# Centring the output weights on chip and dropping the mean from the norms behind them, in a two-layer attention and expert kernel on one core

## The reference, cut to what matters

```python
x = x + layernorm(attention(layernorm(x)))     # linear attention, 16 heads of 8, causal; ends in  values @ Wo + bo
x = x + layernorm(ffn(layernorm(x)))           # ffn = shared expert + top-1 of 16 experts
# shared:  (silu(h @ w_gate.T) * (h @ w_up.T)) @ w_down.T
# expert:  (up * silu(gate)) @ down_proj[e],   gate, up = split(score * h @ gate_up_proj[e])
# layernorm(y) = (y - mean(y)) / sqrt(var(y) + 1e-5), without gain or bias
```

## Time and profile before

| | us |
|---|---|
| median of three runs (lowest, highest) | 351.48 (351.32, 351.48) |
| the profiled execution: its own time | 353.47 |
| its span, first to last instruction | 351.6 |
| VectorE busy | 284.8 (81%) |
| TensorE busy | 266.0 (76%) |
| GpSimd busy | 193.1 (55%) |
| ScalarE busy | 188.8 (54%) |

### The profile page before, as it was taken

One profiled execution on the slowest core, in us unless ns is written; L12 is line 12 of the kernel. 1 busy time (PEld: TensorE's weight loads), 2 busy tenths in 40 slices (PEclk: granted clock), 3 DMA queues, 4 the chain that ended last, 5 costly groups with the idle time before them and its releaser, 6 DMA issues.

```text
span 351.6 us, 6328 instructions
## 1 busy us (share of the span) xinstructions
PE 266.0 (76%) x1493; PEld 189.3 (54%) x1493; DVE 284.8 (81%) x1147; ACT 188.8 (54%) x572; POOL 193.1 (55%) x221
## 2 busy tenths in 40 slices
PE   0449899999999995838887988730999999999100
PEld 0215565565656552524555755520999988988000
DVE  3599999999999999996998786560279999999940
ACT  1723566565656652447666563301799888885000
POOL 5064677777677773300055556371006888888870
PEclk9998999999999999877999899965699999999855
DMA  4999960000000000000011111126960101110100
GB/s 112 334 427 348 352 203 0 2 3 0 2 0 2 2 0 0 1 3 0 0 63 61 62 62 61 62 76 196 358 207 15 34 30 36 39 36 32 31 2 0
DMA packets 20275, 28.60 MB, mean 81 GB/s; under 512 B 2285, under 2 KB 15476, under 8 KB 19856
## 3 DMA queue, kind: packets, MB, share of 16 engines
q1 hardware_dynamic: 16624, 21.57, 18.2%
q0 software_dynamic: 3040, 6.37, 5.3%
q10 hardware_dynamic: 576, 0.26, 0.3%
HBM read 15.57 MB, written 13.60 MB: 83 GB/s over the span
## 4 chain that ended last, share of the span: by engine, by line
PE 39%; DVE 21%; POOL 17%; issue 12%; DMA 5%; ACT 1%; another core or an unknown queue 1%; SPq 1%; POOLq 0%; ACTq 0%; DVEq 0%
PE banks L1019 13%; POOL out L484 10%; POOL rows L478 5%; PE banks L1042 5%; DMA rows<-in_x 4%; PE banks L1106 3%; PE banks L1140 2%; PE banks L1048 2%; DVE hT L824 2%; POOL sorted_rows L468 2%; PE banks L1007 2%; PE banks L1040 1%; PE banks L1065 1%; PE banks L1063 1%; DVE stats L859 1%
## 5 line engine op out<-in xcount | busy, mean ns | idle before, releaser
L443 POOL TENSOR_TENSOR kv<-qk,vv 128x1024 f32<-128x1024 f32 x32 | 62.5, 1952 | 2.5
L1019 PE MATMUL banks<-kv,upto 128*128 128x512 f32 x128 | 61.3, 602 | 0.8 <-POOL kv L443 0.8
L1140 PE MATMUL banks<-xsT,w_now 128*128 128x128 f32 x376 | 53.8, 288 | 0.4 <-issue 0.4
L484 POOL DMA_INDIRECT out<-rows,token_i x47 | 46.9, 998 | 9.6 <-issue 8.0
L437 POOL TENSOR_TENSOR qk<-ex,rl 128x256 f32<-128x256 f32 x32 | 23.3, 729 | 50.4 <-ACT ex L542 50.4
L1140 PEld LDWEIGHTS banks<-xsT,w_now 128*128 128x128 f32 x376 | 48.1, 200 | 1.2 <-issue 0.5
L468 POOL DMA_INDIRECT sorted_rows<-rows,slot_i x32 | 31.6, 986 | 30.2 <-DVE slot_i L814 22.2
L728 DVE TENSOR_TENSOR prod<-banks,qk 128x1024 f32<-128x1024 f32 x32 | 38.9, 1217 | 2.7 <-PE banks L1019 0.8
L750 DVE TENSOR_REDUCE num<-prod 128x128 f32<-128x1024 f32 x32 | 38.7, 1208 | 0.3 <-DVE den L745 0.3
L958 DVE TENSOR_TENSOR hT_e<-silu_e,banks 128x256 f32<-128x256 f32 x47 | 19.3, 412 | 19.6 <-ACT silu_e L619 14.9
L478 POOL TENSOR_TENSOR rows<-rows,yn 128x128 f32<-128x128 f32 x40 | 19.2, 481 | 28.4 <-DVE yn L950 26.6
(11 more groups left out here) (152 smaller groups left out, 660.6 us busy)
## 6 DMA issues: line engine op xcount, KB each, us to landing
sorted_rows<-rows SPq DMA_DIRECT2D x3, 1950.0 KB, 12.0
rows<-sorted_rows SPq DMA_DIRECT2D x11, 520.0 KB, 6.2
w_exp<-in_gate_up SPq DMA_DIRECT2D x4, 1024.0 KB, 9.2
w_exp_down<-in_down SPq DMA_DIRECT2D x8, 256.0 KB, 8.8
out<-rows,token_i POOLq DMA_INDIRECT x47
rows<-in_x SPq DMA_DIRECT2D x1, 512.0 KB, 8.9
sorted_rows<-rows,slot_i POOLq DMA_INDIRECT x32
rows<-sorted_rows SPq DMA_DIRECT2D x1, 390.0 KB, 5.4
```

Of the source, the lines that this page charges most:

```text
L443: nc.gpsimd.tensor_tensor(kv[:, u, :].rearrange("p (h m d) -> p h m d", h=NH, m=HD), k, v, ALU.mult).then_inc(s_kv, 1)
L484: nc.gpsimd.indirect_dma_start(out=out_rows, out_offset=bass.IndirectOffsetOnAxis(ap=token_i[:, j - 1:j], axis=0), in_=rows[:, j - 1, 0:D] ...
L1019: ins = nc.tensor.matmul(ps_s[u % 2][:, cols], upto[:], kv[:, u, cols], start=True, stop=True)
L1140: ins = nc.tensor.matmul(ps_gue[u % 2][:, c * P:(c + 1) * P], w_now[:, u % 2, c * P:(c + 1) * P], xsT[:, u % 2, :], start=True, stop=True)
```

## The change

The means of `bo`, of the rows of `w_o`, of `w_d` and of all `w_exp_down` are subtracted on VectorE by `centre_steps` (a reduction over the 128 columns, then one scalar_tensor_tensor with the sum broadcast). The norm of the attention output and the norm of the ffn output then need only rstd. `ya`, `yn`, `nmean3` and the semaphores `s_ya`, `s_yn`, `s_fin_last` are gone. In stage 2 VectorE does the residual of each tile in one instruction, `x = y * rstd + x`, four of 128x128 in place of two additions of 128x256. In stage 3 it does the same for each output tile, and GpSimd only issues the output DMAs. The norm of a quad is `scale_steps`, 11 instructions in place of 14, and the outputs of a quad are made in the second half of the next quad's steps. The first norm's inputs keep their mean (`nmean2[:, 0]` is still made).

```diff
+def scale_steps(nc, series, st, width, scratch, rs):
+    mean_even, sq_even, sq_odd = st[1], st[2], st[5]
+    ve, y, t = scratch[0:3]
+    series.wait()
+    yield series.done(tensor(t, mean_even, mean_even, ALU.mult))
+    yield series.done(fused(out=ve, in0=sq_even, scalar=width * EPS, in1=sq_odd, op0=ALU.add, op1=ALU.add))
+    series.wait()
+    yield series.done(fused(out=ve, in0=ve, scalar=1.0 / width, in1=t, op0=ALU.mult, op1=ALU.add))
...
+    yield series.done(fused(out=rs, in0=t, scalar=0.5625, in1=y, op0=ALU.add, op1=ALU.mult))
+SCALE_STEPS = 11
+def centre_steps(nc, series, rows_of, sums, ready=None):
+    n, width = rows_of.shape[1], rows_of.shape[2]
+    yield series.done(nc.vector.tensor_reduce(sums, rows_of, AX, ALU.add))
+    series.wait()
+    ins = nc.vector.scalar_tensor_tensor(
+        out=rows_of, in0=sums.rearrange("p (n o) -> p n o", o=1).to_broadcast([P, n, width]), scalar=-1.0 / width,
+        in1=rows_of, op0=ALU.mult, op1=ALU.add)
+    yield ins.then_inc(ready, 1) if ready else ins
...
 # GpSimd, stage 3
-            for j in range(ST + 1):
-                if j < ADDED_BY_POOL:
-                    r = flat(rows[:, j:j + 1, 0:D])
-                    pool.wait_ge(s_yn, j + 1)
-                    nc.gpsimd.tensor_tensor(r, r, yn[:, j % 4, :], ALU.add).then_inc(s_fin, 1)
...
+            for j in range(ST):
+                pool.wait_ge(s_fin, j + 1)
+                nc.gpsimd.indirect_dma_start(
...
 # ScalarE, setup and stage 2
             act.wait_ge(s_bias, 64)
+            act.wait_ge(s_centred_o, 1)
...
-                if live(s + 3, NG):
-                    act.wait_ge(s_norm2, s + 4)
-                    for k in range(GT):
...
-                            ACT.Identity, bias=nmean2[:, 1, c], scale=rstd2[:, 1, c])
...
 # VectorE, setup
             dve.wait_ge(s_x[0], 16)
             setup.done(finish(stats_of(*CHUNKS[0])))
+            dve.wait_ge(s_bias, 64)
+            finish(centre_steps(nc, centring, bias[:, 3 * D:4 * D].rearrange("p (n d) -> p n d", n=1), row_sums[:, 0:1])
+                   ).then_inc(s_centred_o, 1)
...
             left_of_bias(1)
+            dve.wait_ge(s_w, 64)
+            finish(centre_steps(nc, centring, w_o[:].rearrange("p (n d) -> p n d", n=1), row_sums[:, 1:2])
+                   ).then_inc(s_centred_o, 1)
             dve.wait_ge(s_x[1], 16)
...
 # VectorE, stage 2, prepare_steps
-                    for half in range(2):
-                        dve.wait_ge(s_ya, 2 * (s + 2) + 1 + half)
...
+                    dve.wait_ge(s_norm2, s + 3)
+                    for k in range(GT):
+                        t = GT * (s + 2) + k
+                        x1 = flat(rows[:, tiles(t), 0:D])
+                        yield nc.vector.scalar_tensor_tensor(
+                            out=x1, in0=flat(rows[:, tiles(t), D:2 * D]), scalar=rstd2[:, 1, tiles(t)], in1=x1,
+                            op0=ALU.mult, op1=ALU.add).then_inc(s_x1, 1)
...
 # VectorE, attention step 4 and the hand-over
-            run_steps(dve, first_step1, 0, 4, 28, 28, 8, 4)
+            run_steps(dve, first_step1, 0, 4, 28, 4, 8, 4)
+            dve.wait_ge(s_w2, 64)
+            shared = centre_steps(nc, centring, w_d[:], row_sums[:, 0:FC], s_centred_d)
+            step1(4, 0, shared, 1)
+            run_steps(dve, step1, 5, 4, 28, 28, 8, 4)
...
+            dve.wait_ge(s_wexp, 16 * (E // 4) * (1 + FC))
+            for e in range(0, E, 4):
+                ins = finish(centre_steps(nc, centring, w_exp_down[:, e:e + 4, :, :].rearrange("p e c d -> p (e c) d"),
+                                          row_sums[:, e * FC:(e + 4) * FC]))
+            ins.then_inc(s_centred_e, 1)
 # VectorE, stage 3
+            def outputs(q, first, last):
+                dve.wait_ge(s_series3, SQ * (q + 1))
+                for i in range(4 * q + first, min(4 * q + last, ST)):
+                    x1 = flat(rows[:, tiles(i), 0:D])
+                    nc.vector.scalar_tensor_tensor(out=x1, in0=flat(rows[:, tiles(i), D:2 * D]),
+                                                   scalar=rstd3[:, q % 2, i % 4:i % 4 + 1], in1=x1,
+                                                   op0=ALU.mult, op1=ALU.add).then_inc(s_fin, 1)
...
+            for j in range(-4, 4 * QUADS):
+                q, u = j // 4, j % 4
+                step3(q, u)
+                if u == 0 and live(q - 1, QUADS):
+                    norms3 = norm_quad(q - 1, min(4, ST - 4 * (q - 1)), Series(dve, s_series3, SQ * (q - 1)))
+                last = q == QUADS - 1
+                for _ in range(((8, 4, 0, 0) if last else (4, 2, 2, 0))[u]):
+                    next(norms3, None)
+                half = u - (1 if last else 2)
+                if live(q - 1, QUADS) and half in (0, 1):
+                    outputs(q - 1, 2 * half, 2 * half + 2)
+            finish(norm_quad(QUADS - 1, ST - 4 * (QUADS - 1), Series(dve, s_series3, SQ * (QUADS - 1))))
+            outputs(QUADS - 1, 0, 4)
```

More of the change, by code:

```diff
@@ L923, in _, with norm_quad, step3 @@
             nc.vector.tensor_scalar(tile_expert[:], tile_expert[:], E - 1, None, ALU.bitwise_and).then_inc(s_experts, 1)
-            norms3 = {}
-            def step3(q, u, parity):
+            dve.wait_ge(s_wexp, 16 * (E // 4) * (1 + FC))
[3 more added lines that the diff above has]
+            ins.then_inc(s_centred_e, 1)
+            def norm_quad(q, n, norm):
+                c = tiles(4 * q, n)
+                dve.wait_ge(s_stats3, min(4 * (q + 1), ST))
+                yield nc.vector.tensor_scalar(token_i[:, c], rows[:, c, TOKEN], -1.0, float(NTOK), ALU.mult, ALU.add)
+                for ins in scale_steps(nc, norm, [stats3[:, 0:n, k] for k in range(6)], D,
+                                       [scratch3[:, k, 0:n] for k in range(3)], rstd3[:, q % 2, 0:n]):
+                    yield ins
+            def outputs(q, first, last):
[5 more added lines that the diff above has]
+                                                   op0=ALU.mult, op1=ALU.add).then_inc(s_fin, 1)
+            norms3 = iter(())
+            def step3(q, u):
                 j = 4 * q + u
@@ L933, in norm_step @@
                     for _ in range(count):
[L934 to L954 removed]
+                        next(norms3, None)
+                if j > 0:
+                    dve.wait_ge(s_sum, min(j, ST))
                 if live(j + 2, ST):
@@ L964, in step3 @@
                                        flat(rows[:, tiles(j - 1), D:2 * D])).then_inc(s_stats3, 1)
[L965 to L970 removed]
+                if u:
+                    norm_step()
                 if live(j, ST):
@@ L1103, in step2 @@
                     at_least(pe, s_sh_out, s)
+                    if s == 0:
+                        pe.wait_ge(s_centred_d, 1)
                     for k in range(GT):
```

97 lines of the change are left out of this document (32 added, 65 removed).

## The result

The changed kernel takes 368.38 us (median of 4 runs, 367.88 to 370.56); the kernel before took 351.40 beside it. The ratio is 1.0498, 95% interval 1.0455 to 1.0541: slower by 5%, where 336.4 us was forecast. The profiled execution took 367.88 us with a span of 366.0, 14.4 more than the span of before.

What follows compares the result with a forecast made beforehand. Stage 3 was taken as bound by VectorE and GpSimd, each holding the other. Terms -7.8 - 5.8 - 1.7 + 1.2 - 1.0 = -15.1 against 351.48 gave 336.4 us; range 333.5 to 339.5 (0.60), wider 331.5 to 342.5.

Steps and rivals of the forecast that it cites:

- Stage 3, pace: Stage 3's 32 tiles: GpSimd no longer a bound, 1.46 us a tile in place of 1.705; -7.8 us.
- Rival A: Stage 3: VectorE stays the bound at 1.59 us a tile, giving 340.6 us; chance 0.14.
- the terms ahead of stage 3: Before stage 3: setup -1.7 us, w_d centring +1.2, stage 2 -1.0, expert centring nothing.
- Stage 3, end: After the last gate and up products: GpSimd sets the end, 13.5 us in place of 19.3; -5.8 us.
- Setup and w_d: Setup: first attention product at 24.3 us, -1.7; attention step 4: w_d centring delayed by kv, +1.2 us.
- Stage 2: Stage 2: ScalarE's ya goes and four shorter instructions replace two additions; -1.0 us (-2 to +1.5).
- rival B: Setup and attention: kv meets the norms, +1.9 in place of -1.7, and w_d costs +2; 340.8 us, chance 0.12.
- Rival D: Stage 3: each output DMA is held by VectorE's new two-input instruction; 358 us if p = 1.89, chance 0.03.

Runs made afterwards that it cites:

- e10: Kernel before with GpSimd's four additions of a quad first, then its four output DMAs in a row, on chip C: 384.23 us, 1.076 of the kernel before.
- e18: The kernel after, unchanged, run again on chip A: 341.97 us, 0.973 of the kernel before.
- e13: Kernel after with a GpSimd addition ahead of each output DMA but the last seven, without w_d's centring, chip D: 354.26 us, 1.003 of the kernel before.
- e4: Kernel before with GpSimd's four additions of a quad first, then its four output DMAs in a row, on chip A: 352.48 us, 1.003 of the kernel before.
- e1: Kernel after with outputs made one in each step (pairs in the last quad), on chip A: 342.91 us, 0.977 of the kernel before.
- e2: Kernel after with GpSimd starting its output DMAs only when all outputs are made, on chip A: 398.53 us against 350.21 for the kernel before.
- e3: Kernel after with one GpSimd addition of its own ahead of each output DMA but the last seven, on chip A: 350.07 us, 0.9995 of the kernel before.
- e17: Kernel after with every token's index past the output's end, so the same DMAs store nothing, on chip A: 342.67 us against 351.28 for the kernel before.
- e16: Kernel before with all of the change but its part in stage 3, on chip D: 355.24 us, 1.012 of the kernel before.
- e15: Kernel after with outputs sent by SyncE's queue in sorted order, without centring bo and w_o, on chip D: 330.29 us, 0.935 of the kernel before.
- e11: Kernel after with outputs made one in each step (pairs in the last quad), on chip C: 362.38 us, 1.014 of the kernel before.
- e14: Kernel after with one output a step and a GpSimd addition ahead of each output DMA but the last seven, chip D: 354.99 us, 1.005 of the kernel before.
- the first three runs: e1, e2 and e3, variants of the kernel after on chip A: 342.91, 398.53 and 350.07 us.

## Why the prediction was wrong

**The step that failed** is the first, "Stage 3, pace": "GpSimd falls from 1.65 to 1.29 us a tile: no longer a bound." GpSimd is no bound, as said, but I took its DMAs out of the reckoning once it had time for them, and put at nothing, without a reason, what four of them in a row do to the waits of the other engines. On the chips of the comparison, B and C they hold TensorE's signals, and the pace goes to 2.18 and more in place of 1.46: +15.2 us over 32 tiles where -7.8 was forecast, and +2.3 in the stretch ahead of them, where the first row of DMAs falls. The addition L478, which I booked as pure cost (0.48 us a tile), also kept the DMAs 1.66 to 1.85 us apart; e10 takes that distance from the kernel before, and on chip C it stands at 1.076 of it.

**The reckoning of the pace was right where nothing is held.** e18 on chip A: (316.64 - 270.02) / 32 = 1.457 us a tile (1.46 forecast), 46.6 us for the 32 tiles in place of 54.6, which is the -7.8 forecast, to 0.2. VectorE is busy 44.02 of 48 us there, 1.34 a tile, where I had summed 1.38. TensorE is full, as forecast. Rival A (VectorE stays the bound) is out. Yet the whole of e18 is 9.3 us under the kernel before (351.28), not 15.1: -7.9 and -4.9 in stage 3 come to -12.8, and some 3.5 us are lost ahead of them. That 341.97 lies inside the range forecast is in part luck, for the terms ahead of stage 3 were wrong.

**Stage 3, end**: 28.4 before, 23.5 in after's profile and in e18: -4.9 in both, where -5.8 stood (-4.8 to -7). Right in kind, at the edge of its range.

**Setup and w_d.** Forecast -1.7 and +1.2 up to the first attention products. The first product indeed starts at 25.28 in place of 26.62 (24.9 forecast), but the fourth at 41.06 in place of 39.88. I counted only up to the first product; the norms of the last chunk go on through the next three steps and meet `kv` there. The timeline of after, third step of GpSimd's `kv`:

```profile
28.25 1.95 POOL L482 TENSOR_TENSOR kv<-qk,vv 128x1024 f32<-128x1024 f32 x1
...
28.41 1.82 DVE L101 TENSOR_SCALAR scratch<-scratch 128x20 int32<-128x20 int32 x1
```

How many do differs from run to run: over the sixteen profiles with the centrings of `bo` and `w_o` the first product starts from 25.28 to 27.53 (26.2 in the mean) and the fourth from 39.72 to 44.30 (41.7); in the four without them from 26.62 to 26.86 (26.8) and from 39.66 to 41.06 (40.3). So the -1.7 was a gain of 0.6 at the first product and a loss of 1.4 at the fourth, in the mean. The `w_d` step behaved as described, only fuller:

```profile
44.05 1.95 POOL L482 TENSOR_TENSOR kv<-qk,vv 128x1024 f32<-128x1024 f32 x1
...
44.79 1.49 DVE L158 SCALAR_TENSOR_TENSOR w_d<-row_sums,w_d 128x256 f32<-128x256 f32 x1
```

From the fourth product to the fifth 5.30 us in place of 3.93, and from the fifth to the eighth 10.90 in place of 10.53: +1.7 (forecast +1.2, bounds 0 and +2). In e13, without that centring, the two stretches are 3.93 and 10.53 again, to the digit. That the instruction ends 0.28 us behind `kv` (46.28 against 46.00) fits the rule I had cited from the Trainium skill (SBUF — State Buffer, "Who interferes with whom").

**Stage 2.** From the last attention product to the first `hT_e` of stage 3: 97.84 us before, 97.05 after, -0.8 (forecast -1.0). On chip A e4, which has the old stage 2, needs 93.83, while the five kernels with the new one need 93.82 (e18), 96.11 (e1), 96.14 (e2), 96.23 (e3) and 96.28 (e17): nothing to 2.4 us more, within the bounds (-2 to +1.5) in one case of five only. What makes the difference between these five I didn't follow up. All that lies ahead of stage 3 together: forecast -1.5, in the two profiles +1.9. On chip A the first `hT_e` starts at 246.42 in e4 and at 249.50 to 251.44 in the five: +3.1 to +5.0, against one profile of the old code. And e16, which has these parts alone, is 1.012 of the kernel before (353.14 x 0.012 = +4 us; by the interval 1.0 to 7.3). So these terms together have the wrong sign in each of these comparisons. This is the part of rival B that came true.

**Rival D** had the right side by luck, with the wrong mechanism. It had VectorE hold the DMAs; in truth DMAs last 983 ns on average in the slow stage 3 (36 of them), and it is TensorE's signals that wait. The warning "DVE blocks DMA" (the Trainium skill, SBUF — State Buffer) turned my eye to that one direction, of DMAs held by VectorE. The trace has nothing of it: in those 77 us (268 to 345) they last 981 to 984 ns. What speaks of the other direction stood in the trace of before, in stage 2, and no group of mine showed it:

```profile
218.54 1.03 POOL L468 DMA_INDIRECT sorted_rows<-rows,slot_i  x1 [0.36 <-issue]
219.88 0.96 POOL L468 DMA_INDIRECT sorted_rows<-rows,slot_i  x1 [0.30 <-issue]
221.15 0.96 POOL L468 DMA_INDIRECT sorted_rows<-rows,slot_i  x1 [0.30 <-issue]
222.42 0.96 POOL L468 DMA_INDIRECT sorted_rows<-rows,slot_i  x1 [0.30 <-issue]
...
224.38 0.59 ACT L583 COPY rows<-banks 128x512 f32<-128x512 f32 x1 [3.70 <-remote]
224.48 0.17 DVE L781 TENSOR_TENSOR taken<-taken,banks 128x16 f32<-128x16 f32 x1 [3.02 <-remote]
```

Beside a row of four DMAs 1.3 us apart, ScalarE and VectorE both wait over 3 us for results of TensorE and are let go within 0.1 us of each other. By the semaphore events 1.7 and 1.6 us of these waits are lateness of the signal. The change made such rows in stage 3, once a quad.

**Open.** Why chips A and the others differ isn't shown, nor whether a DMA's issuing or its rows' way does the holding: e17 was to tell and ran on the chip without. e15 shows that the same bytes by SyncE's queue hold nothing in an execution whose stage 2 is held; but they go to consecutive rows there, so it parts neither the issuing from the way of scattered rows. Nor is it shown from which distance on DMAs hold: those of e11 do, which stood 1.35 to 1.57 us apart where nothing was held, 1.66 doesn't, and all runs at 1.66 have a GpSimd addition between the DMAs. Nor did I find a complete version that beats the kernel before everywhere: e1 and the kernel after gain 2 to 3% on chip A and lose 1.4% and 4.1% on C, e14 (on D) stays within 0.6% of before; e15's 330.3 us shows what a way out without GpSimd would be worth, but it leaves out the order of the tokens and two centrings.

## What to carry to other kernels

When a change takes work off GpSimd between its software DMAs, the work may have been what kept them apart: count not only who has time for the DMAs but how close they come to each other beside TensorE. A wait that the trace ascribes to nothing ("remote"), or two engines released in the same instant long after the work they wait for, is a sign to price before the change, not after. Where the trace keeps semaphore events, compare their times with the ends of the instructions that cause them. And run the kernel under study on the same chip as its variants: the first three runs had the paces expected on a chip where there was nothing to find.

## What the runs showed of the hardware

- TensorE's completion signals reached ScalarE and VectorE up to 2.95 us late beside GpSimd's indirect DMAs 1.29 us apart in the comparison, and up to 3.85 on B and C; on chip A never over 0.01 us, with the same program: 341.97 us there against 367.88 to 380.30 elsewhere. ScalarE's and VectorE's own signals were at most 0.04 us late in stages 2 and 3 of any run.
- Paces of stage 3 by the distance of the DMAs, where signals are held: 2.18 to 2.51 us a tile in rows of four, at 1.29 or at 1.29, 1.61 and 1.29; 1.98 one to a tile; 1.66 to 1.72 at 1.66 to 1.85; 1.46 by SyncE's queue. With none held, 1.45 to 1.46 for all but those that GpSimd's additions bound (1.67 to 1.70).
- Behind its last DMA GpSimd does a DRAIN of 6.5 us (before, after, e18); in e15, where the last one comes in stage 2, it lies under other work.
- Which kernel is the better one can depend on the chip: the kernel after stands to the kernel before as 0.973 on A, 1.041 on C and 1.064 on B.
